# One variance chain per step, and two weights prepared inside step 0, in a fused RWKV and FFN layer

## The reference

```python
x = x + attention(layernorm(x)); x = x + ffn(layernorm(x))

def attention(x):                          # RWKV, H=32 heads of N=16, chunks of Q=64 tokens
    xx = shift_by_one_token(x) - x
    r, k, v = ((x + xx * maa_m) @ W_m.T for m in "rkv")
    g = silu((x + xx * maa_g) @ Wg.T)
    for each chunk:
        y = ((r @ k) * w_mat) @ v + (r @ state) * wb
        state = ws * state + (k * wk) @ v
    y = (y - mean) / sqrt(var + EPS)       # per token and head of 16 channels
    return (y * gamma + beta) * g @ Wo.T

def ffn(x):                                # 512 -> 2048 -> 512
    return gelu(x @ W0.T + bias0) @ W1.T + bias1
```

## Time and profile before

| | |
|---|---|
| runs | 2166.96 us median of 3 (2165.43 to 2167.08) |
| profiled execution | 2165.32 us, span 2163.5 us |
| busy share of the span | PE 96%, PEld 69%, DVE 87%, ACT 54%, POOL 18% |
| chain that ended last | PE 52%, DVE 31%, issue 5%, SPq 2%, ACT 2% |
| DMA | 452.72 MB, q1 67.9% of 16 engines |

### The profile page before, as it was taken

The page is one execution under the profiler, slowest core; times in us unless marked ns, Lnnn a source line. Parts: engine busy times, 40 slices in busy tenths (PEclk is TensorE's granted clock), DMA queues, the critical chain, the costliest instruction groups (busy, mean ns, idle before and its releaser), DMA issues.

```text
span 2163.5 us, 58680 instructions
## 1 busy us (share of the span) xinstructions
PE 2073.6 (96%) x24056; PEld 1485.2 (69%) x24056; DVE 1874.7 (87%) x4336; ACT 1169.2 (54%) x1940; POOL 378.8 (18%) x331
## 2 busy tenths in 40 slices
PE   5678999999999999999999999999999999999998
PEld 4456677777667777667777766777776677777665
DVE  6888998888899888889988888998888998888861
ACT  6555455565545565545556554555555455565442
POOL 1111112111111211211121111112111112111120
PEclk8889999999999999999999999999999999999999
DMA  6545667776666777666677766667776667777667
GB/s 206 185 145 158 207 200 224 223 228 201 201 204 206 226 229 220 192 201 208 216 228 223 227 183 210 198 218 229 223 224 186 210 201 222 226 225 206 200 214 238
DMA packets 342987, 452.72 MB, mean 209 GB/s; under 512 B 183872, under 2 KB 221248, under 8 KB 342720
## 3 DMA queue, kind: packets, MB, share of 16 engines
q1 hardware_dynamic: 341088, 448.76, 67.9%
q10 hardware_dynamic: 1632, 0.21, 0.1%
HBM read 316.24 MB, written 25.17 MB: 158 GB/s over the span
## 4 chain that ended last, share of the span: by engine, by line
PE 52%; DVE 31%; issue 5%; SPq 2%; ACT 2%; DMA 1%; DVEq 0%; ACTq 0%
PE F L917 13%; PE F L888 12%; PE sc L719 6%; PE YT L747 6%; DVE mixf L227 6%; DVE att L1114 5%; PE B L719 4%; DVE S L1137 4%; PE YT L719 3%; DVE att L1108 3%; DVE mix L287 3%; DVE kv L1123 2%; PE B L868 2%; DVE gT L1144 1%; DVE dx L218 1%
## 5 line engine op out<-in xcount | busy, mean ns | idle before, releaser
L888 PE MATMUL F<-xT,ring 128*128 128x256 f16 x4096 | 484.9, 273 | 9.2 <-ACT hT L1396 3.6
L917 PE MATMUL F<-ring,hT 128*128 128x512 f16 x2016 | 475.3, 379 | 1.4 <-ACT hT L1396 1.4
L888 PEld LDWEIGHTS F<-xT,ring 128*128 128x128 f16 x4096 | 396.2, 98 | 72.5 <-issue 7.4
L917 PEld LDWEIGHTS F<-ring,hT 128*128 128x128 f16 x2016 | 189.6, 98 | 200.6 <-ACT hT L1396 3.3
L283 ACT ACTIVATE mix<-mixf 128x1024 f16<-128x1024 f32 x128 | 135.2, 1056 | 326.9 <-DVE mixf L227 213.8
L1396 ACT ACTIVATE hT<-F,b,f_rho 128x256 f16<-128x256 f32 x512 | 260.5, 565 | 36.4 <-PE F L888 36.2
L227 DVE SCALAR_TENSOR_TENSOR mixf<-dx,maa,xnT 128x256 f32<-128x256 f32 x512 | 270.7, 556 | 0.4 <-PEq L492 0.3
L719 PE MATMUL B<-mix,WT 128*128 128x256 f16 x2304 | 269.6, 274 | 0.0
L1519 POOL TENSOR_TENSOR Shl<-S,Shl 128x512 f16<-128x512 f32 x128 | 153.8, 1202 | 657.2 <-ACT Shl L1363 657.2
L719 PEld LDWEIGHTS B<-mix,WT 128*128 128x128 f16 x2304 | 223.9, 98 | 36.1 <-issue 0.2
L1363 ACT ACTIVATE Shl<-S 128x512 f16<-128x512 f32 x128 | 80.2, 627 | 239.0 <-DVE S L1137 131.9
(11 more groups left out here) (175 smaller groups left out, 3037.5 us busy)
## 6 DMA issues: line engine op xcount, KB each, us to landing
ring<-w_dram SPq DMA_DIRECT2D x512, 512.0 KB, 4.6
kx<-kT SPq DMA_DIRECT2D x96, 256.0 KB, 2.5
rx<-rT SPq DMA_DIRECT2D x96, 256.0 KB, 4.4
xa<-in_L_attn_x SPq DMA_DIRECT2D x32, 512.0 KB, 7.4
vbd<-vN SPq DMA_DIRECT2D x256, 64.0 KB, 2.8
x<-in_L_attn_x SPq DMA_DIRECT2D x32, 512.0 KB, 5.4
out<-x SPq DMA_DIRECT2D x31, 512.0 KB, 3.9
ring<-in_L_ffn_W SPq DMA_DIRECT2D x10, 512.0 KB, 8.5
```

The costliest lines, as they stand in the source:

```text
L888: mm = eng.matmul(F[:, j % 2, i * BT:(i + 1) * BT], ring[:, use % RING, i, a * C + kk * P:a * C + (kk + 1) * P], xT[:, :, kk, :], start=(k ...
L917: mm = eng.matmul(F[:, t, :], hT[:, k, rows(t)], ring[:, use % RING, i, a * C:(a + 1) * C], start=(k == 0 and a == 0), stop=(k == NH - 1 a ...
```

## The change

- **One chain.** The variances of the rows of block n+1, of the heads of block n-1 and of the FFN's rows (block n-2) stand side by side in `rs_a` (68 columns) and go through one chain of 11 instructions in step n. Means and variances of both kinds of rows are in one tile `mv`. The FFN's chain at the end of a step is gone; its statistics stay there (`dve_f_stats`). `act_fnorm` waits for the chain of its own step (`s_mean`).
- **DVE's order.** The last `dve_take_y` of a step stands ahead of the second residual and the FFN's statistics. At the head of a step the mixes fill the places between the chain's instructions; K's remainders stand after its instructions 1 and 6, `mix_lo` after 8 (steps 0 to 2 have K's first remainder and `mix_lo` ahead of the chain).
- **ACT's order.** `act_fnorm` stands behind both halves of K.
- **Preparation.** The block ahead of step 0 prepares K, R and V only, K with a scale of its own. G and O are loaded in four halves into memory that later holds `x1`, `own_f` and `own_y`; ACT squares them at the end of the block, and PE, ACT and DVE prepare them inside step 0 (`pe_late`, `act_late`, `dve_late`), with the factors that need their scale. All eight squares of W0's pieces are in step 0 (three were in the block). The piece at place `R1` of step 0 is moved to `X1`. `ygT`, `yg`, `xT` and `e16` share that memory.
- SP's program for the steps is the same text as before.

```diff
-ORDER = (K_, R_, V_, G_, O_)
-TOGETHER = ((K_, R_), (V_, G_, O_))
+ORDER = (K_, R_, V_)
+TOGETHER = ((K_,), (R_, V_))
+LATE = ((G_, 0), (G_, 1), (O_, 0), (O_, 1))
-PREPARED_AT = (("R1", "V0", "V1", "G0", "sc1", "G1", "sc2", "sc3"),
+PREPARED_AT = (("V0", "V1", "X1", "G0", "sc1", "G1", "sc2", "sc3"),
...
+    def dve_row_var(eng, n):
+        first, last = has(n)
+        if first == ROWS:
+            eng.wait_ge(s_bn, 2 * NT * (n + 2))
+        if last == LATER:
+            eng.wait_ge(s_fbn, 2 * NT * (n - 1))
+        at = of_rows(first, last)
+        eng.tensor_scalar(rs_a[:, :].rearrange("p (k c) -> p k c", k=2)[:, at, 0:NT], mv[:, at, :, 1], LN_EPS, None,
+                          ALU.add).then_inc(s_va, 1)
+    def dve_power_half(eng, n, k):
+        first, last = has(n)
+        if k == 0:
+            eng.wait_ge(s_va, n + 2)
+            if first <= HEADS <= last:
+                eng.wait_ge(s_gn, n)
+        at = slice(EDGES[first], EDGES[last + 1])
+        rsqrt_step(eng, k, s_rs, RSQRT_STEPS * (n + 1), rs_a[:, at], rs_r[:, at], rs_t[:, at])
...
+    def act_late(eng, k):
+        eng.wait_ge(s_lscl, POW2_PER)
+        eng.wait_ge(s_ltr, k + 1)
+        eng.activation(late_part(k, 0), late_psum(k)[:, :, :], ACT.Identity, scale=late_scale_of(k)).then_inc(s_lhi, 1)
+    def dve_late(eng, k):
+        eng.wait_ge(s_lhi, k + 1)
+        eng.scalar_tensor_tensor(out=late_part(k, 1), in0=late_psum(k)[:, :, :], scalar=late_scale_of(k),
+                                 in1=late_part(k, 0), op0=ALU.mult, op1=ALU.subtract).then_inc(s_llo, 1)
...
     def dve_step(eng, n):
+        if n <= nb + 1:
+            if early:
+                mixing(G)
+            if ahead:
+                dve_stats(eng, n + 1, 0)
+            mixing(1)
+            if tail:
+                dve_variance(eng, n - 1, 1)
+            if ahead:
+                dve_stats(eng, n + 1, 1)
...
+            if ahead:
+                for t in range(NT):
+                    dve_mean_var(eng, n + 1, t)
+            mixing(1)
+            if tail:
+                dve_head_var(eng, n - 1)
+            dve_row_var(eng, n)
+            if att_n and early:
+                mix_lo(eng, n, 2)
+            mixing(1)
+            for k in range(RSQRT_STEPS):
+                dve_power_half(eng, n, k)
+                if att_n:
+                    if k == 1 and not early:
+                        dve_K_lo(eng, n, 0)
+                    elif k == 6:
+                        dve_K_lo(eng, n, 1)
+                    elif k == 8 and not early:
+                        mix_lo(eng, n, 2)
+                    else:
+                        mixing(1)
+            dve_row_mean(eng, n)
...
+            if tail:
+                for t in range(NT):
+                    dve_normalized(eng, n - 1, t)
...
+            dve_take_y(eng, n, 1)
         if tail:
             dve_residual(eng, n - 1, 1)
-            dve_fln(eng, n - 1)
-        if att_n:
-            dve_take_y(eng, n, 1)
+            dve_f_stats(eng, n - 1)
...
     def act_fnorm(eng, f):
-        eng.wait_ge(s_fln, LN_PER * (f + 1))
+        eng.wait_ge(s_mean, f + 4)
...
+    def act_step0(eng, squares):
+        for j in range(3):
+            act_piece_square(eng, 0, j, squares)
+        act_K_hi(eng, 0, 0)
+        act_late(eng, 0)
+        act_mix_hi(eng, 0, 2)
+        act_K_hi(eng, 0, 1)
+        act_late(eng, 1)
+        act_piece_square(eng, 0, 3, squares)
+        act_R_hi(eng, 0, 0)
+        act_late(eng, 2)
+        act_mix_hi(eng, 0, 3)
+        act_R_hi(eng, 0, 1)
+        act_piece_square(eng, 0, 4, squares)
+        act_late(eng, 3)
+        for j in range(5, PIECES):
+            act_piece_square(eng, 0, j, squares)
```

More of the change, by code:

```diff
@@ new lines, in program, with dve_stats, dve_mean_var @@
+    s_fbn, s_xh, s_fx, s_up, s_h, s_dn, s_e, s_o = (
+        sem(f"s_{v}") for v in ("fbn", "xh", "fx", "up", "h", "dn", "e", "o"))
+    ROWS, HEADS, LATER = range(3)
+    EDGES = (0, NT, NT + NT * H, 2 * NT + NT * H)
+    def dve_stats(eng, n, t):
+        if t == 0:
+            eng.wait_ge(s_xa, 16 * (n + 1))
+        eng.bn_stats(bn[:, t, :], xa[:, t, :]).then_inc(s_bn, 1)
+    def dve_mean_var(eng, n, t):
+        eng.wait_ge(s_bn, 2 * NT * n + t + 1)
+        eng.bn_aggr(mv[:, 0, t, :], bn[:, t, :]).then_inc(s_bn, 1)
@@ new lines, in has, with of_rows @@
+    def has(n):
+        first = ROWS if n + 1 < nb else HEADS if n <= nb else LATER
+        last = LATER if n >= 2 else HEADS if n >= 1 else ROWS
+        return first, last
+    def of_rows(first, last):
+        return slice(int(first > ROWS), 1 + int(last == LATER))
+    def dve_row_var(eng, n):
[7 more added lines that the diff above has]
+                          ALU.add).then_inc(s_va, 1)
@@ L347, in dve_power, with sp_late, act_late_square @@
         op.then_inc(done, 1)
+    late_raw = [x1[:, 0, :, :].rearrange("p t c -> p (t c)"), own_f[:, :, :].rearrange("p a c -> p (a c)"),
+                own_y[:, 0, :], own_y[:, 1, :]]
+    late_raw = [v.rearrange("p (b c) -> p b c", b=G) for v in late_raw]
+    def sp_late(eng, k):
+        u, half = LATE[k]
+        eng.dma_start(late_raw[k], weights[u].rearrange("(b p) c -> p b c", p=P)[:, :, 2 * P * half:2 * P * half + 2 * P]
+                      ).then_inc(s_late[k], 16)
+    def act_late_square(eng, k, squares):
+        eng.wait_ge(s_late[k], 16)
+        if due(k):
+            eng.wait_ge(s_lsq, k)
+        eng.activation(squares, late_raw[k].rearrange("p b c -> p (b c)"), ACT.Square,
+                       accum_out=late_sum[:, k:k + 1]).then_inc(s_lsq, 1)
@@ new lines, in late_psum, with pe_late, late_part, late_scale_of @@
+    def late_psum(k):
+        return Y if k == 1 else F
+    def pe_late(eng, k):
+        if k >= 2:
+            eng.wait_ge(s_llo, 1 if k == 2 else 3)
+        for i in range(2):
+            for b in range(G):
+                tr = eng.transpose(late_psum(k)[:, i, rows(b)], late_raw[k][:, b, rows(i)], ident[:, :])
+        tr.then_inc(s_ltr, 1)
+    def late_part(k, a):
+        u, half = LATE[k]
+        return WT[:, u, a, 2 * half:2 * half + 2, :]
+    def late_scale_of(k):
+        return late_scl[:, LATE[k][0] - G_:LATE[k][0] - G_ + 1]
@@ L370, in prepare @@
         tp = (tp4[:, 0, :, :], tp4[:, 1, :, :], Y)
-        landed = [own.enter_context(nc.semaphore(f"landed{u}")) for u in range(5)]
+        landed = [own.enter_context(nc.semaphore(f"landed{u}")) for u in range(len(ORDER))]
         s_tab, s_sum, s_all, s_tr, s_hi, s_lo = (
@@ L744, in pe_V @@
             eng.wait_ge(s_yi if t else s_y, NT * n)
+        else:
+            eng.wait_ge(s_llo, 2)
         for i, (a, b) in enumerate(PASSES):
```

289 lines of the change are left out of this document (134 added, 155 removed).

## The result

The changed kernel takes 2203.19 us (median of 4 runs, 2201.61 to 2204.22) against 2167.02 before (4 runs, 2165.43 to 2168.71): 1.0166 times as long, 95% interval 1.0149 to 1.0184. The profiled execution spans 2202.4 us, 38.9 more than before; that is more than the medians differ (36.2), because the profiled run of before was 1.7 under its median and that of after 1.0 above.

The account below looks back on a forecast made before the run. TensorE (PE), busy nearly throughout, was taken as the bound. Steps 3 to 30 +31, start +2.5, step 1 -1, step 2 +1 and end +3 sum to +36.5: 2203.5 us for the runs, range 2174 to 2236.

Parts of the forecast that it names:

- (a): Steps 3 to 30: `kx` waits behind the later `xh` transpose on SP's queue; 2203.5 us, range 2180 to 2225, chance 0.62.
- (c): Rival, steps 3 to 30: landings hardly move, 0 to +0.2 a step; 2163 to 2178 us, chance 0.12.
- (d): Rival, steps 3 to 30: `xh` ends by +14.2, `kx` goes out as today, steps keep 63.46; 2161 us, chance 0.10.
- Landings moved by 2.0: Steps 3 to 30: transposes issued 1.55 us later on SP's queue land 2.0 later, bounds +0.3 and +3.2.
- 1.1 a step: Steps 3 to 30: each grows by 1.1 us over the mean of 63.46, +31 in 28 steps, bounds +6 and +62.
- The price of the join: ACT's wait for the transposed words of x (L275): start moves from +31.57 to about +33.5, costing 1.1 to 1.3 a step.
- Both meet at L1114, so the larger counts: At DVE's last `att` difference, late words of x and PE's 1.0 wait for ring unit 5 overlap; only the larger costs.
- Part of the price through POOL: Steps 3 to 30: POOL's three instructions slide over the `att` differences on a shared port, about 1.3 a step.
- rival (b): Steps 3 to 30: the DMA queue's work decides, landings move 3.2, +2.1 a step; 2232 us, chance 0.16.
- The start, +2.5 and -1: Block saves 5.8 but step 0 takes the work back, sum +2.5 (bounds -4 and +7); step 1's head -1.
- Step 2, +1: Step 2's first `up`, earlier in its step than later ones, waits for the later `xh`, about +1.
- The end, +3: Step 32: `xh` is ready later and SP issues the weights behind its transpose, at 2094.0 instead of 2091.03: +3.

Follow-up runs that it names:

- e2: The kernel before, with SP's transpose of `xh` in steps 2 to 31 also waiting for K's remainder, so `kx` goes behind it: 2196.35 us, ratio 1.0132.
- e1: The kernel after, with `kx` and `kN` issued ahead of the transpose of `xh` on SP's queue in steps 2 to 31: 2172.91 us, ratio 1.0016.
- e3: The kernel after, with the FFN's variance in its own chain of 13 small instructions again at the end of the step: 2165.66 us, ratio 0.9985.
- e5: The kernel after, with the ring's weight unit 5 issued right behind the words of x: 2199.46 us, ratio 1.0147.
- e10: The kernel after, with POOL's two `yg` subtractions cut to 8 of 128 columns and PE reading the high part instead: 2193.78 us, ratio 1.0117.
- e12: The kernel after, with the words of x ahead of the ring's unit 4 and unit 5 right behind unit 4: 2173.64 us, ratio 1.0027.
- e4: The kernel after, with five weight units of step 32 issued ahead of the transpose of `xh`: 2205.46 us, ratio 1.0178.
- e6: The kernel after, with the words of x issued ahead of the ring's unit 4: 2181.16 us, ratio 1.0059.
- e7: The kernel after, with 20 unread matmuls filling PE's idle time before the first `up` of step 32: 2201.78 us, ratio 1.0163.
- e11: The kernel before, with DVE's two K remainders after chain steps 4 and 8 instead of 6 and 13: 2162.23 us, ratio 0.9977.

## Why the prediction was right, point by point

The forecast was 2203.5 and the median is 2203.19; the mechanism is the forecast one, (a). That the totals agree to 0.3 us is luck: the profiled executions differ by 38.9 where the sum had 36.5, and the medians by 36.2. Landings moved, so (c) was not the case, and the transpose of `xh` went at +15.57, so (d) was not either. The steps:

- **SP's order is the mechanism.** Shown from three sides: e2 makes the loss in the kernel before, e1 takes it away in the kernel after by the order alone, e3 by giving the FFN its own chain back. Transpose forecast at +15.8, found at +15.57; `kx` at +17.1, found at +16.94. (The last four chain steps, the mean and `mix_lo` add up to 2.4 with the slots given, not to 2.2; it changes nothing here.) The shift was 1.43 and not 1.55.
- **Landings moved by 2.0.** Mis-sized: the words of x landed at +32.87 against +31.45, 1.4 later, which is the shift of the issue. The reason I gave for 2.0 (the engines stand idle until `xh` comes) was not needed.
- **1.1 a step.** Measured 1.11, in part by offsetting errors. The price of the join was taken from one disturbed step of before, 0.45 for 1.06; in truth there is a reserve of about 0.6 from +31.57 on and then 1 for 1. By that law the forecast join of +33.5 would have cost 1.3; it came at +32.97. The wait for unit 5 was forecast at 1.0, measured 0.87, with landings 1.5 later instead of 2.0: the unit landed at +38.0 in the mean of before, not at +37.7, and single steps wait up to 2.2. "Both meet at L1114, so the larger counts" fits e5, e10 and e12: each alone is about 0.8, the larger of both in each step 1.08. The lower clock behind two of the waits, 0.12 a step, was not in the sum.
- **Part of the price through POOL.** Shown by e10: without POOL's two long subtractions DVE's stretch is 1.15 shorter. Not all of this is a price of the late join: in an undisturbed step two mixes beside POOL already take 2.30 instead of 0.87, 1.4 lost; in late ones the mixes take 2.02 and the differences 2.24 instead of 1.29, 2.1 lost. So lateness adds about 0.7. The Trainium skill (SBUF — State Buffer, "SBUF: two separate sides") says that of a GpSimd instruction that reads SBUF and a DVE instruction with two SBUF inputs the one that starts first gets the shared port pair for its whole instruction. The trace agrees: in late steps the first `att` difference starts behind POOL's subtraction for the state and takes 1.64, and alone it takes 0.68. The forecast from this rule, 1.3 a step, was for landings 2.0 later.
- **The DMA queue's work, rival (b).** Not the cause of the loss: landings moved with the issue (1.4 for 1.5), and e1's did. But where the order in the queue changes, landings move too: in step 32 the transpose behind two units under way lands 2.3 later (e4), and the words with one unit less ahead of them land 0.9 sooner after their issue (e6), 0.4 of it because the issue itself is shorter. The Trainium skill (DMA: Bandwidth & Descriptors, "Issuing engines are not separate DMA queues") says that issuing is usually small beside the transfer. Here it is not: one transpose of the words holds SP for 3.9 to 6.1 (4.7 on average in the kernel after), of 7.4 from its issue to its landing, and that is what everything behind it waits for.
- **The start, +2.5 and -1.** The first DVE instruction behind the barrier is at 41.60, not at 40.2: V's hi part is ACT's at 34.91, and the four squares are 1.24 each and end at 40.78. So the block gives back 4.4 and not 5.8. `vw` of step 0 starts at 67.89, against 67.4. The sum to the mark of step 1 was +1.5; measured +2.2 in this trace, and 2.7 as the mean of nine traces (183.7) over the mean of four with the old preparation (181.0). Mis-sized by a microsecond, and no gain: what the block saves, step 0 takes back and more.
- **Step 2, +1.** The wait for `xh` is there (5.73 before the first `up`), but a later wait of 3.08 for ACT's first GELUs, which the kernel before has at +25.7 of this step, is gone in return: +0.4.
- **The end, +3.** The first `up` came 2.74 later, as forecast. The step that failed is that nothing else would follow: after a pause of 4.77 PE ran at the lower clock and lost another 2.2, so +5.2. The size varies from trace to trace: the four kernels with the old step 32 have tails of 80.7 to 82.7, the eight with the new one (without e7) 84.8 to 86.0, 4.2 apart in the mean.

## What to carry to other kernels

Instructions saved on an engine that would have waited anyway gained nothing here, and the result that they delayed stood at the head of an in-order queue: before merging chains, list what waits behind each result on the issuing engine, and let the queue's order follow the order in which things become ready (e1: 1.5% back from one exchange on SP's queue). One disturbed step is not a price list: set the length of many steps beside the landing, and look for the point from which lateness costs one for one. When two things are late by the same cause, undoing one shows little (e5) and says nothing against it.

## What the runs showed of the hardware

A pause of PE can cost twice, once by itself and once by the granted clock behind it. In the kernel after, step 21 (mark 1403.02) has one pause of 2.02 for the ring and takes 66.77, 3.5 over the floor: behind the pause the next group of 16 matmuls takes 2.93, where each such group takes 1.9 elsewhere, and the window around it has a granted clock of 0.90:

```profile
1443.79 2.93 PE L989 MATMUL F<-own_f,ring 128*128 128x256 f16 x16 [2.02 <-DMA ring<-w_dram]
...
1435.00:1452.00 17.00, 14.98 (x207) 12.25 (x206) 16.39 (x29) 11.20 (x18) 3.75 (x3) 0.90 0.87 281
```

Step 25 is alike (a wait of 1.89, 66.65). But step 6 has a pause of 2.18 and takes 65.27, no more than the waits explain, and e3 has nearly the same two pauses in step 32 as the kernel before, 1.45 and 0.80 (0.95 in before), and yet a granted clock of 0.74 in the window around them, where before has 1.00; its tail is 2.6 longer. In e11, whose step 32 is the code of before, the pauses are 1.45 and 1.15, and the window of the 4 us behind them shows 0.57:

```profile
2090.28:2094.28 4.00, 4.00 (x22) 2.95 (x23) 0.00 (x0) 0.44 (x1) 1.15 (x2) 0.57 1.03 374
```

Its tail is 2.0 longer than that of the kernel before. In steps 3 to 30 of all fourteen traces the five pauses of 2.31 to 2.52 were each followed by the lower clock; of the fourteen of 1.80 to 2.22, five were. So the length of the pause alone does not decide. What does stays open. In steps 21 and 25 the slower matmuls make 1.7 each, 3.3 together, of the 31 us of the steady steps.
